# Layer with a clipped scan on one core: the D term written into PSUM by VectorE, the product ring widened, and one buffer for x and the residual

## The chip, the cores and the metric

The kernel runs on one core of one Trainium2 chip. The metric is the device time of one execution in microseconds (us), the median of several runs. The core has a matrix engine (TensorE, PE in the profile; PEld is its weight load), VectorE (DVE), ScalarE (ACT), GpSimd (POOL) and SyncE (SP), which here only issues DMAs. They work side by side, each in its own order of instructions, and wait for one another on semaphores.

## The reference

Input x is 2 x 2048 x 512. Each sequence goes through the same layer, and the result is added to x:

```python
xr, gate = jnp.split(x @ W_in.T, 2, axis=-1)          # 1024 channels each
xr = xr + t_emb[:, None, :]
xc = silu(causal_conv_of_4_taps(xr) + b_conv)
xn = (xc - mu) / jnp.sqrt(var + 1e-05) * ln_g + ln_b
Bm, Cm, dt = jnp.split(xn @ W_xproj.T, 3, axis=-1)    # 16 states each
dt = jnp.tanh(dt @ W_dt.T + b_dt) * 0.01
A = -jnp.tanh(A_log)
Ad = 1.0 + dt * A
Bd = Bm * jnp.minimum(jnp.linalg.norm(xn, axis=-1, keepdims=True), 1.0)
def step(h, inputs):                                   # over 2048 time steps
    h = jnp.clip(h * ad[:, :, None] + bd[:, :, None] * xt[:, None, :], -10.0, 10.0)
    yt = jnp.einsum('bd,bdh->bh', ct, h)
y = ys + D * xn
return x + y * jax.nn.silu(gate) @ W_out.T
```

The change touches the line of `D * xn`.

## The kernel before

Time is cut into 32 chunks of 128 steps (`STEPS`), the two sequences in turn. Body `k` works on chunk k and, beside it, finishes chunk k-1 and prepares chunks k+1 and k+2. A body has 32 steps `s` (`TILES`), one for each pair of a block of 128 channels (`u`, 8 of them) and a group of 4 states (`q`, 4 of them). A tile goes through the engines as follows. TensorE writes the unclipped states into a bank of `ps_fill` (`fill`, L542, three steps ahead), ScalarE copies them to `low` (L779), TensorE adds the width of the clip (`widen`, L551), VectorE runs the clipped scan from `low` and the bank into `ks` (L990), GpSimd multiplies by C into `prod` (`weigh`, L1088), and TensorE adds the product into `ps_y`, transposed (`flip`, L578, `LAG` = 4 steps behind). `ps_y` is a single bank of 512 channels. Tiles 0 to 15 make the first half of y, tiles 16 to 31 the second. Flips 0 and 1, and 16 and 17, are issued as pairs in steps 5 and 21.

A half of y begins with `base` (L558), a matmul with `start=True`. The D term is added by `skip` (L564): GpSimd multiplies xn by D into `xd`, which shares the buffer of `xc` (L1045, after tile 11), and TensorE adds each half of `xd` through the identity, the first half at flip 12, the second at flip 16. Each of these f32 matmuls is two records in the trace. After flips 15 and 31 VectorE multiplies the bank by the gate (`gated`, L978). The next `base` waits for that (`y_gated`). A product buffer of the ring `prod` (`HOLD` = 4) is written again only after its flip.

Beside the tiles TensorE works off jobs. Step s has two points, 2s (before its flip) and 2s+1 (behind it). The table `JOBS`, written by hand, gives for each job the first point, the number of points over which it is spread, the chunk and the bank of `ps_job` (the last number). `TAKE` gives the point at which ScalarE or VectorE empties the bank, and a job waits until the one before it on its bank has been taken. The jobs are: z, zT and nb (the small projections), gate and xr (the input projection), conv and xt, h0, hend and carry (states between chunks), yT (the gated y transposed) and out (the output projection). The carry jobs end in ScalarE's copies to `xh` and `lend` (L755, L757) and VectorE's `xl` (L970), which frees the bank. `GATED_AT` gives the points of the two gate products on VectorE.

SP issues all DMAs in one order: x transposed into `xf` at the body's start (wanted by ScalarE at point 13, step 6), the residual into `res` at once behind it (wanted at point 53), then the stacks, C and bounds, and at the end the store of the chunk from `res`.

## Time and profile before

| | us |
|---|---|
| median of 3 runs | 2132.08 |
| lowest and highest | 2129.33, 2132.22 |
| the profiled execution's own time | 2132.36 |
| its span | 2130.6 |
| its PE busy | 1991.3 |
| its POOL busy | 1799.5 |
| its DVE busy | 1659.2 |
| its ACT busy | 1421.1 |

The profile is of one execution. Busy times of TensorE contain the overlap of one matmul's tail with the next, so the chain of waits, which walks from start to start, shows smaller steps than the durations of the instructions. A release named "issue" is idle time for which the profile shows no other engine.

### The profile page before, as it was taken

Reading aid. Unit: us, or ns where it says so; the run is one execution under the profiler, and the core shown is the slowest. Engines: PE = TensorE matmul, PEld = TensorE weight load, DVE = VectorE, ACT = ScalarE, POOL = GpSimd, SP = SyncE. Lnnn points to the kernel's source line nnn. Section 1 sums busy time; section 2 is a strip of 40 time slices with the busy share of each in tenths; the row PEclk is TensorE's granted clock in tenths of the full one; section 3 lists DMA queues with packets and bytes.
Section 4 is the critical chain, followed back from the end, with each engine's and each line's share of the span. In section 5 each row is a group of like instructions: output and inputs, shape, how many; then the busy total and the mean of one; then the engine's idle time right before and its main releaser. Section 6 shows DMA issues by size and latency. Waiting matters only on the chain.

```text
span 2130.6 us, 47194 instructions
## 1 busy us (share of the span) xinstructions
PE 1991.3 (93%) x16976; PEld 1471.4 (69%) x16976; DVE 1659.2 (78%) x2108; ACT 1421.1 (67%) x3462; POOL 1799.5 (84%) x1444
## 2 busy tenths in 40 slices
PE   5699999999999999999999999999999999999988
PEld 5466777776777776777776777676676777677765
DVE  3477887787887787887787888787888787888796
ACT  4676766776766676766676766676766677766643
POOL 1389898888898888898888898888898888898886
PEclk8699999999999999999999999999999999999999
DMA  5121112121112121112111111211111112121110
GB/s 171 54 59 49 53 43 60 57 61 49 53 42 61 57 59 50 54 44 60 56 58 50 54 50 54 57 56 54 51 57 47 57 56 58 47 59 44 54 49 16
DMA packets 81993, 118.09 MB, mean 55 GB/s; under 512 B 21840, under 2 KB 50896, under 8 KB 77088
## 3 DMA queue, kind: packets, MB, share of 16 engines
q1 hardware_dynamic: 81760, 115.07, 18.7%
q8 instruction: 135, 2.21, 0.4%
q14 instruction: 98, 0.80, 0.1%
HBM read 59.96 MB, written 9.18 MB: 32 GB/s over the span
## 4 chain that ended last, share of the span: by engine, by line
PE 69%; ACT 17%; issue 8%; DVE 4%; POOL 1%; SPq 1%; DMA 0%; ACTq 0%; DVEq 0%; POOLq 0%
PE ps_y L578 13%; PE ps_job L493 8%; PE ps_fill L551 8%; PE ps_job L447 8%; PE ps_fill L542 7%; PE ps_job L452 7%; PE ps_job L465 5%; ACT low L779 4%; PE ps_y L558 3%; PE ps_job L459 2%; PE ps_job L474 2%; ACT tap L738 2%; ACT xh L672 2%; ACT gate L666 2%; PE ps_y L564 1%
## 5 line engine op out<-in xcount | busy, mean ns | idle before, releaser
L1088 POOL TENSOR_TENSOR prod<-ks,crep 128x512 f32<-128x512 f32 x1024 | 1283.6, 1272 | 226.4 <-PE ps_y L578 214.9
L990 DVE TENSOR_TENSOR_SCAN ks<-low,ps_fill 128x512 f32<-128x512 f32 x1024 | 1211.5, 1205 | 228.6 <-PE ps_fill L551 224.6
L779 ACT COPY low<-ps_fill 128x512 f32<-128x512 f32 x1024 | 585.4, 581 | 540.6 <-PE ps_fill L542 536.4
L578 PE MATMUL ps_y<-c_sb,prod 128*128 128x128 f32 x4096 | 610.7, 274 | 2.4 <-POOL prod L1088 1.1
L578 PEld LDWEIGHTS ps_y<-c_sb,prod 128*128 128x128 f32 x4096 | 462.0, 142 | 94.1 <-issue 63.3
L542 PEld LDWEIGHTS ps_fill<-ts,xs 128*128 128x128 f16 x4096 | 316.4, 98 | 165.7 <-issue 5.0
L542 PE MATMUL ps_fill<-ts,xs 128*128 128x128 f16 x4096 | 397.9, 220 | 6.4 <-DVE ks L990 4.2
L551 PE MATMUL ps_fill<-spans,pick 128*128 128x512 f16 x1024 | 391.6, 382 | 9.8 <-ACT low L779 6.8
L738 ACT ACTIVATE tap<-xr,cols_sb 128x128 f32<-128x128 f32 x768 | 252.1, 394 | 16.3 <-PE ps_job L465 16.2
L447 PE MATMUL ps_job<-x,w_in 128*128 128x128 f16 x3072 | 215.7, 221 | 14.6 <-POOL x L1058 7.8
L452 PE MATMUL ps_job<-w_in,x 128*128 128x512 f16 x768 | 209.7, 383 | 10.9 <-ACT gate L666 10.9
L493 PE MATMUL ps_job<-w_out,yT 128*128 128x512 f16 x768 | 206.4, 379 | 1.8 <-DVE yT L901 1.5
L447 PEld LDWEIGHTS ps_job<-x,w_in 128*128 128x128 f16 x3072 | 188.0, 99 | 25.0 <-issue 20.8
L465 PE MATMUL ps_job<-c_sb,tap 128*128 128x128 f32 x1024 | 157.4, 278 | 24.9 <-issue 16.9
L551 PEld LDWEIGHTS ps_fill<-spans,pick 128*128 128x128 f16 x1024 | 100.2, 98 | 74.8 <-ACT low L779 23.5
L465 PEld LDWEIGHTS ps_job<-c_sb,tap 128*128 128x128 f32 x1024 | 118.2, 144 | 42.9 <-issue 22.3
L738 ACT ACTIVATE tap<-xr,conv_b,cols_sb 128x128 f32<-128x128 f32 x256 | 123.5, 482 | 0.0
L452 PEld LDWEIGHTS ps_job<-w_in,x 128*128 128x128 f16 x768 | 71.8, 104 | 48.7 <-issue 17.0
L970 DVE SCALAR_TENSOR_TENSOR xl<-xh,c_sb,ps_job 128x512 f16<-128x512 f16 x64 | 47.8, 747 | 68.8 <-ACT lend L757 68.8
L493 PEld LDWEIGHTS ps_job<-w_out,yT 128*128 128x128 f16 x768 | 69.8, 98 | 35.4 <-DVE yT L901 1.7
L1036 POOL TENSOR_TENSOR xn<-xn,row_g 128x1024 f32<-128x1024 f32 x32 | 75.5, 2359 | 5.5 <-ACT xn L654 5.5
L1045 POOL TENSOR_TENSOR xc<-xn,row_d 128x1024 f32<-128x1024 f32 x32 | 75.4, 2355 | 0.0
(125 smaller groups left out, 2269.7 us busy)
## 6 DMA issues: line engine op xcount, KB each, us to landing
crep<-c_dram SPq DMA_DIRECT2D x32, 1024.0 KB, 4.8
xs<-xh SPq DMA_DIRECT2D x256, 64.0 KB, 2.0
xs<-xl SPq DMA_DIRECT2D x224, 64.0 KB, 2.0
xf<-in_xT SPq DMA_DIRECT2D x32, 256.0 KB, 2.7
res<-in_x SPq DMA_DIRECT2D x32, 256.0 KB, 2.6
out_dram<-res SPq DMA_DIRECT2D x32, 256.0 KB, 2.1
ts<-tth SPq DMA_DIRECT2D x128, 32.0 KB
ts<-tth SPq DMA_DIRECT2D x128, 31.0 KB
```

The source lines that it names most:

```text
L447: last = mm(ps[:, e * P:(e + 1) * P], w_in[:, a, c, d:d + P], x16[:, q, b, c, :], start=(c == n == 0), stop=(c == CB - 1 and n == 2))
L452: last = mm(ps, x16[:, q, a, c, :], w_in[:, b, c, DI + i * BANK:DI + (i + 1) * BANK], start=(c == n == 0), stop=(c == CB - 1 and n == 2))
L465: last = mm(ps[:, e * P:(e + 1) * P], tap[:, d % TAPRING, v], ident, start=(v == 0), stop=(v == TAPS - 1), is_transpose=True)
L493: last = mm(ps, yT[:, a, c, :], w_out[:, b, c, :], start=(c == n == 0), stop=(c == DB - 1 and n == 2))
L542: last = mm(o[:, :, SUB * jj:SUB * (jj + 1)], xs[:, p, jj, u * P:(u + 1) * P], ts[:, p, jj, q * QN * SUB:(q + 1) * QN * SUB].rearrange("s ...
L551: mm(ps_fill[:, (TILES * k + s) % RING], pick[:], spans[:, p, q * BANK:(q + 1) * BANK], start=False, stop=True, skip_group_check=True).the ...
L578: last = mm(ps_y[:, cut], prod[:, s % HOLD, e, :], ident, start=False, stop=(u % 4 == 3 and q == 3 and e == QN - 1), is_transpose=True)
L738: last = act_fn(tap[:, d % TAPRING, v], xr[:, p, d, v:v + P], ACT.Identity, scale=cols[:, d, 3 + v:4 + v], bias=conv_b[:, p, d:d + 1] if v ...
L779: copy(low[:, (TILES * k + s) % RING], ps_fill[:, (TILES * k + s) % RING]).then_inc(sem["low_copied"], 1)
L990: nc.vector.tensor_tensor_scan(ks[:, u % 2, QN * q:QN * (q + 1)].rearrange("d n t -> d (n t)"), low[:, g % RING], ps_fill[:, g % RING], 0. ...
L1036: tt(xn[:, p], xn[:, p], row_g[:], ALU.mult).then_inc(sem["xg"], 1)
L1088: tt(prod[:, i % HOLD], ks[:, u % 2, part], crep[:, p, part], ALU.mult).then_inc(sem["weighed"], 1)
```

## The change

The D term is written by VectorE. A new `skip` on VectorE multiplies half of xn by D and writes the result straight into `ps_y`, right behind each gate product (points 39 and 8); TensorE's `base` waits for it (`skip_set`) and adds to it with `start=False`. One matmul of zeros at the program's start opens the bank. GpSimd's product, the buffer `xd` and TensorE's two skip matmuls are gone. `HOLD` is 5, and the ring is counted through all chunks. In steps 5 and 21, the jobs of the second point come before the pair of flips and the base. `res` is a view of `xf`: the load of x waits for the store before it, the residual's load for `xT_low`, and it moves behind the xl stack loads in SP's order. Some jobs move in the tables.

```diff
-HOLD = 4
+HOLD = 5
-        xd = xc
-        res = sb("res", [P, DM])
+        res = xf[:].rearrange("p c t -> p (c t)")
...
-        TAKE = {("z", 0): 5, ("gate", 0): 7, ("hend", 0): 6, ("hend", 1): 8, ("yT", 1): 10, ("gate", 1): 12,
+        TAKE = {("z", 0): 5, ("gate", 0): 7, ("hend", 0): 6, ("hend", 1): 7, ("yT", 1): 12, ("gate", 1): 12,
...
-        GATED_AT = (39, 7)
+        GATED_AT = (39, 8)
...
+                    if k >= 2:
+                        sp.wait_ge(sem[f"out_done{p}"], 16 * ((k - p) // 2))
                     sp.dma_start(xf[:], xT_dram[b, :, :, bass.ds(c * P, P)]).then_inc(sem["xT_in"], 16)
...
+                if exists(k, -1):
+                    b, c = chunk(-1)
+                    if exists(k, 2):
+                        sp.wait_ge(sem["xT_low"], k + 3)
+                    elif k >= 2:
+                        sp.wait_ge(sem[f"out_done{p}"], 16 * ((k - p) // 2))
+                    sp.dma_start(res, x_dram[b, bass.ds(c * P, P), :]).then_inc(sem["res_in"], 16)
...
+            mm(ps_y[:], pick[:], spans[:, 0, 0:BANK], start=True, stop=True).then_inc(sem["y_opened"], 1)
...
-                since(pe, "y_gated", 2 * k + i)
-                mm(ps_y[:], mT[:, p], xn[:, p, half], start=True, stop=False)
-
-            def skip(k, p, i):
-
-                if i == 0:
-                    pe.wait_ge(sem["xd_done"], k + 1)
-                last = mm(ps_y[:], ident, xd[:, i * BANK:(i + 1) * BANK], start=False, stop=False)
-                if i == 1:
-                    last.then_inc(sem["xd_used"], 1)
+                pe.wait_ge(sem["skip_set"], 2 * k + i + 1)
+                mm(ps_y[:], mT[:, p], xn[:, p, half], start=False, stop=False, skip_group_check=True)
...
+                    if len(tiles) == 2:
+                        jobs_at(k, p, 2 * s + 1)
...
+            def skip(k, p, i):
+
+                half = slice(i * BANK, (i + 1) * BANK)
+                dve.wait_ge(sem["xn_done"], k + 1)
+                since(dve, "y_gated", 2 * k + i)
+                if k == i == 0:
+                    dve.wait_ge(sem["y_opened"], 1)
+                tt(ps_y[:], xn[:, p, half], row_d[:, half], ALU.mult).then_inc(sem["skip_set"], 1)
...
                             gated(k, p, 0)
+                            skip(k, p, 1)
...
-                        tt(xd[:], xn[:, p], row_d[:], ALU.mult).then_inc(sem["xd_done"], 1)
```

The other moved jobs, by their first points: yT 1 from 10 to 12, carry 0 from 32 to 33, carry 1 from 36 to 38, out from 40 in 13 parts to 42 in 12, yT 0 from 54 to 56, hend 1 from 8 to 7.

What that makes of TensorE's order in steps 19 to 21, first before. The rows begin behind the second carry job and flip 14 (`ps_y<-c_sb,prod` is a flip, `ps_job<-c_sb,tap` a part of conv, `ps_job<-w_out,yT` of out, `ps_fill<-spans,pick` a widen and `ps_fill<-ts,xs` a fill).

```order
L551 MATMUL ps_fill<-spans,pick 128x512
L542 MATMUL ps_fill<-ts,xs 128x4x32 x4
L465 MATMUL ps_job<-c_sb,tap 128x128 x4
L578 MATMUL ps_y<-c_sb,prod 128x128 x4
L551 MATMUL ps_fill<-spans,pick 128x512
L542 MATMUL ps_fill<-ts,xs 128x4x32 x4
L465 MATMUL ps_job<-c_sb,tap 128x128 x4
L493 MATMUL ps_job<-w_out,yT 128x512 x3
L551 MATMUL ps_fill<-spans,pick 128x512
L542 MATMUL ps_fill<-ts,xs 128x4x32 x4
L558 MATMUL ps_y<-xn,mT 128x512
L564 MATMUL ps_y<-xc,c_sb 128x512
```

The same steps of the changed kernel, from the end of the second carry job on:

```order
L483 MATMUL ps_job<-xh,bqm 128x512
L572 MATMUL ps_y<-c_sb,prod 128x128 x4
L555 MATMUL ps_fill<-spans,pick 128x512
L546 MATMUL ps_fill<-ts,xs 128x4x32 x4
L469 MATMUL ps_job<-c_sb,tap 128x128 x4
L555 MATMUL ps_fill<-spans,pick 128x512
L546 MATMUL ps_fill<-ts,xs 128x4x32 x4
L469 MATMUL ps_job<-c_sb,tap 128x128 x4
L497 MATMUL ps_job<-w_out,yT 128x512 x3
L562 MATMUL ps_y<-xn,mT 128x512
L572 MATMUL ps_y<-c_sb,prod 128x128 x8
```

The wait of out (before: ahead of the conv part that precedes L493; after: ahead of the one that precedes L497) now stands behind two widens and fills and a conv part that stood in part behind it, and the skip is gone.

TensorE in steps 3 to 5, before, from flip 31 on (`ps_job<-w_in,x` is gate, `ps_job<-c_sb,kend` hend, `ps_job<-c_sb,gate` yT):

```order
L578 MATMUL ps_y<-c_sb,prod 128x128 x4
L551 MATMUL ps_fill<-spans,pick 128x512
L542 MATMUL ps_fill<-ts,xs 128x4x32 x4
L452 MATMUL ps_job<-w_in,x 128x512 x3
L483 MATMUL ps_job<-c_sb,kend 16x128 x4
L452 MATMUL ps_job<-w_in,x 128x512 x3
L551 MATMUL ps_fill<-spans,pick 128x512
L542 MATMUL ps_fill<-ts,xs 128x4x32 x4
L452 MATMUL ps_job<-w_in,x 128x512 x3
L487 MATMUL ps_job<-c_sb,gate 128x128 x4
L558 MATMUL ps_y<-xn,mT 128x512
```

and after:

```order
L572 MATMUL ps_y<-c_sb,prod 128x128 x4
L487 MATMUL ps_job<-c_sb,kend 16x128 x4
L555 MATMUL ps_fill<-spans,pick 128x512
L546 MATMUL ps_fill<-ts,xs 128x4x32 x4
L456 MATMUL ps_job<-w_in,x 128x512 x6
L555 MATMUL ps_fill<-spans,pick 128x512
L546 MATMUL ps_fill<-ts,xs 128x4x32 x4
L456 MATMUL ps_job<-w_in,x 128x512 x6
L562 MATMUL ps_y<-xn,mT 128x512
```

Hend 1 is ahead of the gate job, yT 1 comes after the base, and the gate's fourth part before it.

VectorE from the scans of step 18 to its step 21, before and after (`ks<-low,ps_fill` is a scan, `gate<-ps_y,gate` the gate product, `ps_y<-xn,row_d` the new skip):

```order
L970 SCALAR_TENSOR_TENSOR xl<-xh,c_sb,ps_job 128x512
L990 SCALAR_TENSOR_TENSOR ks<-low,ps_fill 128x512 x2
L970 SCALAR_TENSOR_TENSOR xl<-xh,c_sb,ps_job 128x512
L990 SCALAR_TENSOR_TENSOR ks<-low,ps_fill 128x512
L978 TENSOR_TENSOR gate<-ps_y,gate 128x512
L990 SCALAR_TENSOR_TENSOR ks<-low,ps_fill 128x512 x5
```

```order
L967 SCALAR_TENSOR_TENSOR xl<-xh,c_sb,ps_job 128x512
L996 SCALAR_TENSOR_TENSOR ks<-low,ps_fill 128x512 x2
L975 TENSOR_TENSOR gate<-ps_y,gate 128x512
L984 TENSOR_TENSOR ps_y<-xn,row_d 128x512
L967 SCALAR_TENSOR_TENSOR xl<-xh,c_sb,ps_job 128x512
L996 SCALAR_TENSOR_TENSOR ks<-low,ps_fill 128x512 x5
```

The gate product and the skip now stand ahead of the second xl.

## Rows read from the trace of the kernel before

**Rows 1.** The page: busy time by engine, and the chain by engine.

```profile
PE 1991.3 (93%) x16976; PEld 1471.4 (69%) x16976; DVE 1659.2 (78%) x2108; ACT 1421.1 (67%) x3462; POOL 1799.5 (84%) x1444
PE 69%; ACT 17%; issue 8%; DVE 4%; POOL 1%; SPq 1%; DMA 0%; ACTq 0%; DVEq 0%; POOLq 0%
```

**Rows 2.** Waits (total us, times, longest), then the base's line (durations, first and last).

```profile
ACT low L779 <- PE ps_fill L542: 536.4, 439, 5.0
...
PE ps_y L558 <- DVE gate L978: 1.7, 2, 1.4
...
L558 PE MATMUL ps_y<-xn,mT x128: 592/593/697, 109.8 to 2098.3; 128*128 128x512 f32 x128
```

**Rows 3.** Busy us by stretch: PE, PEld, DVE, ACT, POOL, clock, DMA share.

```profile
998.70:1062.70 64.00, 61.39 (x533) 45.50 (x532) 51.40 (x66) 43.92 (x108) 56.45 (x47) 1.00 0.20 55
...
1018.00:1031.50 13.50, 12.17 (x88) 8.24 (x86) 11.43 (x15) 13.22 (x36) 10.63 (x10) 1.00 0.27 89
```

**Rows 4.** Groups (busy us, mean ns), then min/median/max ns of two VectorE lines.

```profile
L564 PE MATMUL ps_y<-xc,c_sb 128*128 128x512 f32 x128 | 65.4, 593 | 1.2 <-POOL xc L1045 1.2
L978 DVE TENSOR_TENSOR gate<-ps_y,gate 128x512 f32<-128x512 f32 x64 | 42.8, 669 | 0.1
L990 DVE TENSOR_TENSOR_SCAN ks<-low,ps_fill 128x512 f32<-128x512 f32 x1024 | 1211.5, 1205 | 228.6 <-PE ps_fill L551 224.6 <-issue 0.2
L1088 POOL TENSOR_TENSOR prod<-ks,crep 128x512 f32<-128x512 f32 x1024 | 1283.6, 1272 | 226.4 <-PE ps_y L578 214.9 <-DVE ks L990 11.3
L1045 POOL TENSOR_TENSOR xc<-xn,row_d 128x1024 f32<-128x1024 f32 x32 | 75.4, 2355 | 0.0
...
L910 DVE TENSOR_TENSOR zm<-z,zm x32: 178/801/805, 55.6 to 2023.5; 1x32 f16<-1x32 f32 x32
...
L945 DVE TENSOR_TENSOR bc<-zT,pf x32: 403/587/2007, 63.0 to 2033.1; 16x256 f32<-16x256 f32 x32
```

**Rows 5.** Chain of waits, 1028 to 1033 us: start, step, what.

```profile
1028.48 0.65 PE ps_job L493 x3
1029.13 0.21 PE ps_fill L551
1029.34 0.22 PE ps_fill L542 x4
...
1030.64 0.86 PE ps_y L564 x2
1031.50 0.88 PE ps_y L578 x8
```

**Rows 6.** Timeline, TensorE, 1027 to 1034 us: start, duration, [idle before].

```profile
1027.85 0.63 PE L465 MATMUL ps_job<-c_sb,tap 128*128 128x128 f32 x4 [0.59 <-issue]
...
1033.30 0.38 PE L551 MATMUL ps_fill<-spans,pick 128*128 128x512 f16 x1
```

**Rows 7.** Timeline, ScalarE and VectorE in the same steps.

```profile
1017.93 0.59 ACT L779 COPY low<-ps_fill 128x512 f32<-128x512 f32 x1 [0.81 <-PE ps_fill L542]
...
1026.30 0.57 ACT L757 COPY lend<-ps_job 16x512 f32<-16x512 f32 x1
...
1023.37 0.75 DVE L970 SCALAR_TENSOR_TENSOR xl<-xh,c_sb,ps_job 128x512 f16<-128x512 f16 x1 [1.42 <-ACT lend L757]
...
1027.01 0.75 DVE L970 SCALAR_TENSOR_TENSOR xl<-xh,c_sb,ps_job 128x512 f16<-128x512 f16 x1 [0.65 <-ACT lend L757]
```

**Rows 8.** Timeline at the chunk's head.

```profile
999.01 0.58 ACT L660 CAST yT<-ps_job 128x512 f16<-128x512 f32 x1 [0.50 <-PE ps_job L487]
...
1000.42 3.73 POOL L1088 TENSOR_TENSOR prod<-ks,crep 128x512 f32<-128x512 f32 x3 [1.43 <-PE ps_y L578]
...
1003.39 0.80 DVE L910 TENSOR_TENSOR zm<-z,zm 1x32 f16<-1x32 f32 x1 [0.56 <-ACT zm L685]
...
1006.30 0.10 PEld L551 LDWEIGHTS ps_fill<-spans,pick 128*128 128x128 f16 x1 [0.28 <-ACT low L779]
...
1059.28 0.81 PE L452 MATMUL ps_job<-w_in,x 128*128 128x512 f16 x3 [0.34 <-ACT gate L666]
```

More of the change, by code:

```diff
@@ L198, in build @@
         JOBS = [(3, 2, "z", 0, 1, 1, 1), (3, 4, "gate", 0, 0, 2, 0), (6, 1, "hend", 0, -1, 2, 1),
-                (8, 4, "gate", 1, 0, 2, 0), (8, 1, "hend", 1, -1, 2, 1), (10, 1, "yT", 1, -1, 2, 1),
+                (8, 4, "gate", 1, 0, 2, 0), (7, 1, "hend", 1, -1, 2, 1), (12, 1, "yT", 1, -1, 2, 1),
                 (15, 1, "zT", 0, 1, 1, 1), (19, 4, "xr", 0, 2, 2, 0), (21, 1, "h0", 0, 1, 2, 1),
                 (24, 4, "xr", 1, 2, 2, 0), (24, 1, "h0", 1, 1, 2, 1), (27, 1, "nb", 0, 1, 1, 1),
-                (33, 11, "conv", 0, 2, 2, 0), (32, 1, "carry", 0, 1, 2, 1), (36, 1, "carry", 1, 1, 2, 1),
-                (40, 13, "out", 0, -1, 1, 1), (46, 9, "conv", 1, 2, 2, 0), (54, 1, "yT", 0, 0, 2, 1),
+                (33, 11, "conv", 0, 2, 2, 0), (33, 1, "carry", 0, 1, 2, 1), (38, 1, "carry", 1, 1, 2, 1),
+                (42, 12, "out", 0, -1, 1, 1), (46, 9, "conv", 1, 2, 2, 0), (56, 1, "yT", 0, 0, 2, 1),
                 (57, 1, "xt", 0, 2, 2, 0), (60, 1, "xt", 1, 2, 2, 0)]
         LAST = {(name, i): first + parts - 1 for first, parts, name, i, *_ in JOBS}
-        TAKE = {("z", 0): 5, ("gate", 0): 7, ("hend", 0): 6, ("hend", 1): 8, ("yT", 1): 10, ("gate", 1): 12,
+        TAKE = {("z", 0): 5, ("gate", 0): 7, ("hend", 0): 6, ("hend", 1): 7, ("yT", 1): 12, ("gate", 1): 12,
                 ("zT", 0): 15, ("h0", 0): 21, ("h0", 1): 24, ("xr", 0): 23, ("nb", 0): 27,
-                ("xr", 1): 28, ("carry", 0): 32, ("carry", 1): 36, ("conv", 0): 44, ("out", 0): 53,
-                ("conv", 1): 55, ("yT", 0): 54, ("xt", 0): 58, ("xt", 1): 62}
+                ("xr", 1): 28, ("carry", 0): 33, ("carry", 1): 38, ("conv", 0): 44, ("out", 0): 54,
+                ("conv", 1): 55, ("yT", 0): 56, ("xt", 0): 58, ("xt", 1): 62}
         TAP_AT = [24, 26, 32, 36, 39, 42, 45, 49]
         Z_AT = 12
-        GATED_AT = (39, 7)
+        GATED_AT = (39, 8)
         BANK_OF = {(name, i): b for _, _, name, i, _, _, b in JOBS}
@@ L321, in body @@
                     later_loads()
-                if exists(k, -1):
-                    b, c = chunk(-1)
-                    if not (isinstance(k, int) and k < 2):
-                        sp.wait_ge(sem[f"out_done{p}"], 16 * ((k - p) // 2))
-                    sp.dma_start(res[:], x_dram[b, bass.ds(c * P, P), :]).then_inc(sem["res_in"], 16)
                 if exists(k, 1):
@@ L394, in body @@
                     sp.wait_ge(sem["out_taken"], k)
-                    sp.dma_start(out[b, bass.ds(c * P, P), :], res[:]).then_inc(sem[f"out_done{b}"], 16)
+                    sp.dma_start(out[b, bass.ds(c * P, P), :], res).then_inc(sem[f"out_done{b}"], 16)
             steps(body)
@@ L414, in _ @@
             pe.wait_ge(sem["gw_ready"], 2)
+            pe.wait_ge(sem["spans_clear"], 3)
             for i, src in enumerate((gw, bw)):
@@ L572, in flip @@
                     base(k, p, s // (4 * NQ))
-                if s in (3 * NQ, 4 * NQ):
-                    skip(k, p, s // NQ - 3)
                 pe.wait_ge(sem["weighed"], TILES * k + s + 1)
@@ L577, in flip @@
                 for e in range(QN):
-                    last = mm(ps_y[:, cut], prod[:, s % HOLD, e, :], ident, start=False,
-                              stop=(u % 4 == 3 and q == 3 and e == QN - 1), is_transpose=True)
+                    last = mm(ps_y[:, cut], prod[:, (TILES * k + s) % HOLD, e, :], ident, start=False,
+                              stop=(u % 4 == 3 and q == 3 and e == QN - 1), is_transpose=True,
+                              skip_group_check=True)
                 last.then_inc(sem["flipped"], 1)
@@ L609, in body @@
                             flip(k - 1, 1 - p, t + TILES)
-                    jobs_at(k, p, 2 * s + 1)
+                    if len(tiles) < 2:
+                        jobs_at(k, p, 2 * s + 1)
             steps(body)
@@ L743, in side @@
                     since(act, "xa", k + 2)
-                    since(act, "xd_used", k + 1)
                     act_fn(xc[:, i * BANK:(i + 1) * BANK], bank("conv", i), ACT.Silu).then_inc(sem["conv_taken"], 1)
@@ L906, in side @@
                     dve.wait_ge(sem["res_in"], 16 * k)
-                    stt(res[:], bank("out"), 1 / WS, res[:], ALU.mult, ALU.add).then_inc(sem["out_taken"], 1)
+                    stt(res, bank("out"), 1 / WS, res, ALU.mult, ALU.add).then_inc(sem["out_taken"], 1)
                 if point == Z_AT + 1 and exists(k, 1):
@@ L1003, in body @@
                             gated(k, p, 0)
+                            skip(k, p, 1)
                         if point == GATED_AT[1] and exists(k, -1):
                             gated(k - 1, 1 - p, 1)
+                        if point == GATED_AT[1] and exists(k, 0):
+                            skip(k, p, 0)
                         side(k, p, point)
@@ L1087, in weigh @@
                 since(pool, "flipped", g - HOLD + 1)
-                tt(prod[:, i % HOLD], ks[:, u % 2, part], crep[:, p, part], ALU.mult).then_inc(sem["weighed"], 1)
+                tt(prod[:, g % HOLD], ks[:, u % 2, part], crep[:, p, part], ALU.mult).then_inc(sem["weighed"], 1)
             steps(body)
```

6 lines of the change are left out of this document (1 added, 5 removed).

## The prediction

> **What bounds the kernel now.** I read the page first, then the waits, the busy time by stretch, the chain of waits, and the timeline of one chunk. The page puts TensorE at 93%, and the chain that ended last is 69% TensorE and 17% ScalarE [rows 1]. The waits say the same from the other side: ScalarE waits 536 us for the fills of TensorE [rows 2], and VectorE 225 us for its widening matmuls [rows 4]. So TensorE is late and the others wait for it. The first and last base matmul stand at 109.8 and 2098.3 us, 31.5 chunks apart, so a chunk takes 63.1 us [rows 2]. The chunk that I read closely runs from 998.7 to 1062.7 us. In it TensorE is busy for 61.4 us of 64 at the full clock (1.00), GpSimd 56.5, VectorE 51.4, ScalarE 43.9 [rows 3]. No other engine has a full chunk of work, but each has full stretches. From 1018 to 1031.5 us ScalarE is busy 13.22 us of 13.5 and TensorE only 12.17 [rows 3]. What a cut on TensorE is worth has to be read there, and at the chunk's head.
>
> **The D term leaves TensorE.** A skip matmul is recorded as two instructions; the chain walks over the pair in 0.86 us (the 593 ns of one record overlap the next) [rows 4, 5]. Two skips in each of 32 chunks: 64 x 0.86 = 55 us, or 1.72 us a chunk. The order of the changed kernel shows none left, so this work is certainly gone. Whether the time goes too is taken stretch by stretch, for one chunk.
>
> **Tail, steps 16 to 21: -1.6 us.** ScalarE starts this run when a fill arrives at 1017.93 (it had waited 0.81 us) and is busy until it has written the second lend, at 1026.30 plus about half a microsecond [rows 7]. VectorE then makes the second xl at 1027.01, having waited 0.65 us for it, and only that frees the bank for out [rows 7]: TensorE resumes at 1027.85 after 0.59 us of waiting [rows 6]. The first skip stands inside this run, so removing it alone moves nothing past 1027.85; I keep that time for both kernels. What counts is what TensorE still has to do behind it. Before: from 1027.85 to the next widen at 1033.30, 5.45 us [rows 6]: a conv part, an out part, widen and fill, base, skip, two flips, a conv part, an out part. After: out starts at 42 and carry 1 at 38, so the conv part, the widen and the fill come ahead of the wait. Behind it stand a conv part (four transposes, as in a flip) 0.44, an out part 0.65, base 0.86, two flips 0.88, and, one step later, the second out part 0.65: 3.48 us by the steps of the chain, the base taken as long as a skip, which has the same shape [rows 5]. Gain 5.45 - 3.48 = 1.97, say 1.9, since some of the gaps at the base may stay. Thus moved work, not the first skip's absence as such, is what turns the saving into time.
>
> Against it stands VectorE's new order: gate, skip, and only then the second xl. VectorE's gate product takes 0.67 us [rows 4]. No row shows a 128x512 product of two SBUF tensors into PSUM. Lower bound: the gate product's 0.67, also 512 elements. Upper bound: two SBUF inputs seem to wait for GpSimd. The 1x32 zm takes 178 ns at best and 801 ns at the median, the 16x256 bc 403 at best, 587 at the median and 2007 at worst [rows 4]. In the chunk read, the three products that GpSimd began at 1000.42 end at 1004.15 and zm, begun at 1003.39, ends at 1004.19 [rows 8]. One whole product of 1.27 us [rows 4] in front makes 1.94 us. I take the middle, 1.3 us, since GpSimd is busy 56 of 64 us and an instruction meets it half way through on average. Now the place of the skip: the first xl frees the bank at 1023.37 + 0.75 [rows 7]; carry 1 (0.65) and flip 15 (0.44) follow, so flip 15 ends near 1025.4, the gate product near 1026.1 and the skip near 1027.4. The lend ends near 1027.1 (1026.30 plus 0.57 and its signal) in both kernels: xl starts 0.3 us later. Tail: -1.9 + 0.3 = -1.6 us.
>
> The Trainium skill has a rule on this ("SBUF — State Buffer", section "SBUF: two separate sides"): a VectorE op with two SBUF inputs and a GpSimd op that reads SBUF exclude each other for the whole instruction, where sharing would cost only a part. The end of zm with GpSimd's products agrees. By the rule at its worst case the sum would be rival (c)'s.
>
> **Head, steps 3 to 10: +0.15 us.** Count from the end of flip 31. TensorE after: hend 1 0.44, widen and fill 0.43, two gate parts 1.30, widen and fill 0.43, two gate parts 1.30: it asks for the base at 3.9 us. Hend 1 now stands ahead of the gate job, where TensorE waited 0.34 us for ScalarE [rows 8], and fills that: -0.34. VectorE has in that time: the wait for hend 1 (0.6, with the tail of a matmul), then each row's duration less some 0.06 us of overlap: its h product 0.6 (512 elements like the gate product), scan 5 1.15, gate 0.6 [rows 4], and the skip 1.3: 4.25 us, with its signal 4.3. So the base waits 0.4 us; with the skip at 0.67 it doesn't wait, at 1.94 it waits 1.0. Before, the base waited only in 2 of 64 places, 1.7 us in all [rows 2]: this is the wait the change adds. Behind it stand the flips, and GpSimd's products behind them. The yT 1 job leaves this stretch (-0.44) for step 6, and its ScalarE cast (0.58 us, in a place where ScalarE was idle afterwards [rows 8]) goes to the front of a run that ends in TensorE's wait for a low copy at 1006.30, 0.28 us [rows 8]. That run grows by about the 0.5 us of the cast: +0.1 net. Sum: -0.34 + 0.4 + 0.1 = +0.16.
>
> **The rest, each at nothing, and its cover.** GpSimd loses a 2.36 us product a chunk [rows 4] and gains at most two blocks of 0.67 us by the skips; it is not on the chain (1%) [rows 1]. The fifth product buffer lets it run one product, 1.27 us, ahead across the base; flips waited for products too rarely to gain by it. The xT load now waits for the store of the block before, and is wanted only in step 6 of the next chunk; the residual load goes behind the xl stack loads, in step 7, and is wanted in step 27. The SP queue is held at neither, since their conditions were met by the waits ahead of them; were it held, the c and bound transfers behind would be late. Putting yT 0 at 56 and its VectorE half behind the statistics shifts 0.6 us between steps without adding any. The opening matmul happens once.
>
> **Sum.** -1.6 + 0.16 = -1.44 us a chunk; x 32 = -46 us. From the profiled execution's own 2132.36 us (median of the runs 2132.08, so no correction): 2086 us, -2.2%.
>
> **Rivals.** (a) The first skip's time is lost: ScalarE's run slips behind TensorE's new start, or out's wait is reached no later relative to it, and only 0.86 us of the pair comes through. Then -0.58 us a chunk, 2114 us. For it: 13.22 of 13.5 us busy. Against: the jobs moved ahead of the wait. (b) More comes back: VectorE's skips at 0.67 us (no 0.3, no 0.4), giving -2.1 us, 2064 us, and with half of the gap of 0.59 us at out gone too [rows 6], 2055. (c) Nothing: both skips meet a whole product, 1.94 us. Then the tail gains 0.95 and the base at the head waits 1.0: -0.2 us a chunk, 2126 us. That is also what the skill's rule of whole-instruction exclusion gives if each skip comes just behind a product's start. (d) Slower: the D term as a link in the y chain. If each skip takes what the worst bc took, 2.0 us, plus 0.3 for twice the elements (half of the gate's 0.67), the base waits 1.4 us and xl is 1.3 us late: -1.9 + 1.3 - 0.24 + 1.4 = +0.56 us a chunk, 2150 us. It decides from a skip of about 2.0 us on. Against it: bc's median is 0.59, and near the base GpSimd often waits for flips.  That the change doesn't do what it says is excluded by the order.
>
> **Chances.** The forecast's case, 2070 to 2102, 58%; (a) 16%; (b) 12%; (c) 6%; (d) 8%. The range takes in the forecast, most of (a) and the upper part of (b): 2062 to 2118. A difference of 0.2% (4 us) is about what the runs can tell. Faster by more than that 86%, within it 6% ((c) in its upper part, or with a little more of a wait), slower 8%.
>
> **What would show it.** TensorE's busy time down by about 55 us in its lines; VectorE up by 64 skips, 43 us if free and 83 us at 1.3 each; GpSimd down 75. The skip's row: near 0.67, 1.3 or 1.9 us decides between (b), the forecast and (c). The waits: base for skip at the head some 0.4 us in each chunk, none at the tail. If the wait at out grows past the 0.59 us, (a) is right. The forecast is wrong if ScalarE's run from 1018 us doesn't keep its length, or if a wait shows at the base of both halves.

## The result and the profile after

The changed kernel is slower. Its median is 2165.4 us (2164.62 to 2165.97, 4 runs) beside 2132.15 us for the kernel before on the same chip (2129.33 to 2132.42). The ratio is 1.016 (95% interval 1.0141 to 1.0176). The profiled execution spans 2164.2 us; its TensorE clock was granted at 0.983 on average. The forecast was 2086 us.

First the page of the changed kernel: busy time by engine, the chain that ended last, and three groups of instructions (busy us, mean ns of one, idle time before them).

```profile
PE 1937.6 (90%) x16849; PEld 1447.2 (67%) x16849; DVE 1751.9 (81%) x2172; ACT 1419.2 (66%) x3462; POOL 1728.9 (80%) x1412
...
PE 64%; ACT 14%; issue 11%; DVE 8%; POOL 1%; SPq 1%; DMA 1%; ACTq 0%; DVEq 0%; POOLq 0%
...
L1091 POOL TENSOR_TENSOR prod<-ks,crep 128x512 f32<-128x512 f32 x1024 | 1284.3, 1276 | 274.2 <-PE ps_y L572 217.5
...
L984 DVE TENSOR_TENSOR ps_y<-xn,row_d 128x512 f32<-128x512 f32 x64 | 108.1, 1688 | 6.6
...
L562 PE MATMUL ps_y<-xn,mT 128*128 128x512 f32 x128 | 72.7, 652 | 28.7 <-DVE ps_y L984 28.7
```

The work moved as planned. TensorE is 54 us less busy than in [rows 1], GpSimd 71 us less, and VectorE 93 us more. But the kernel didn't end earlier: TensorE now waits more than it saved. The skip's mean is 1.69 us; 0.67 would have been free of contention and 1.3 was assumed. The base matmul, which hardly waited before [rows 2], waits 28.7 us.

The waits say where (us in total, times, longest). PE and PEld are two queues of one engine, and a wait usually stands in both; the PE row is the one to add up.

```profile
ACT low L776 <- PE ps_fill L546: 617.2, 462, 7.4
...
PE ps_job L469 <- issue: 64.4, 28, 2.3
...
PE ps_y L562 <- DVE ps_y L984: 28.7, 28, 3.4
...
PE ps_job L491 <- DVE xf L904: 14.7, 31, 0.9
...
PE ps_job L487 <- DVE h L891: 13.1, 31, 0.4
```

ScalarE waits 81 us more for fills than in [rows 2], so TensorE is what is late. TensorE's own waits that are new or longer are four, each in nearly every chunk: 2.3 us ahead of the conv part that stands before out, 0.9 us at the head's base, and two of 0.4 to 0.5 us which the forecast didn't have, at yT (L491) and at hend (L487). A fifth, small one stands at the z job (L474): 0.22 us in 30 chunks, 6.5 us in all; its row is the last of the head's below.

Now the tail, steps 16 to 21 of one chunk, in the timeline (start, duration, idle before and what ended it). The first row is the start of ScalarE's run, and so matches the first of [rows 7]; the others follow in order of time.

```profile
1031.09 0.58 ACT L776 COPY low<-ps_fill 128x512 f32<-128x512 f32 x1 [0.81 <-PE ps_fill L546]
...
1037.20 2.32 DVE L996 TENSOR_TENSOR_SCAN ks<-low,ps_fill 128x512 f32<-128x512 f32 x2
...
1039.44 0.67 DVE L975 TENSOR_TENSOR gate<-ps_y,gate 128x512 f32<-128x512 f32 x1
...
1039.60 0.57 ACT L754 COPY lend<-ps_job 16x512 f32<-16x512 f32 x1
...
1040.12 1.27 POOL L1091 TENSOR_TENSOR prod<-ks,crep 128x512 f32<-128x512 f32 x1
...
1040.21 1.75 DVE L984 TENSOR_TENSOR ps_y<-xn,row_d 128x512 f32<-128x512 f32 x1
...
1041.87 0.74 DVE L967 SCALAR_TENSOR_TENSOR xl<-xh,c_sb,ps_job 128x512 f16<-128x512 f16 x1
...
1042.71 0.63 PE L469 MATMUL ps_job<-c_sb,tap 128*128 128x128 f32 x4 [2.31 <-issue]
...
1045.55 0.38 PE L555 MATMUL ps_fill<-spans,pick 128*128 128x512 f16 x1
```

The second lend starts 8.51 us after the run's start, 8.37 us before: ScalarE's run kept its length. Its data are there at about 1040.2, but VectorE is in the skip, and xl comes at 1041.87 without having waited for anything. Before, VectorE had waited 0.65 us for the same lend [rows 7]. GpSimd's product at 1040.12 starts 0.09 us ahead of the skip, and the skip ends 0.57 us behind that product's end at 1041.39. TensorE resumes 11.62 us after the run's start; before it was 9.92 us [rows 6, 7]. From there to the next widen it takes 2.84 us (1045.55 - 1042.71) where it took 5.45 [rows 6].

The head, steps 3 to 10 of the same body:

```profile
1007.17 0.60 PE L487 MATMUL ps_job<-c_sb,kend 128*16 128x128 f32 x4 [0.42 <-DVE h L891]
...
1010.30 1.82 DVE L984 TENSOR_TENSOR ps_y<-xn,row_d 128x512 f32<-128x512 f32 x1
...
1010.30 1.26 POOL L1091 TENSOR_TENSOR prod<-ks,crep 128x512 f32<-128x512 f32 x1
...
1012.17 1.13 PE L562 MATMUL ps_y<-xn,mT 128*128 128x512 f32 x2 [0.93 <-DVE ps_y L984]
...
1016.59 0.49 PE L474 MATMUL ps_job<-c_sb,z 128*16 128x128 f32 x3 [0.22 <-DVE yT L898]
```

Skip and product start in the same hundredth of a microsecond. The product takes its plain 1.26 us, and the skip takes 1.82: it too ends 0.56 us behind the product's end.

The next chunk's head is the counter-example, one of three in this trace: here the skip started first, by 0.01 us, and GpSimd's product is the one that is stretched.

```profile
1075.09 0.70 DVE L984 TENSOR_TENSOR ps_y<-xn,row_d 128x512 f32<-128x512 f32 x1
...
1075.10 1.80 POOL L1091 TENSOR_TENSOR prod<-ks,crep 128x512 f32<-128x512 f32 x1
```

### The profile page after: what moved, and what is told of

It is laid out like the page before. It is cut to its first block, busy times and chain, and to the rows that moved or that the text cites. A ratio compares the mean times of both kernels' runs of the same rounds, so it can differ in the third digit from the quotient of the medians.

```text
span 2164.2 us, 47005 instructions
## 1 busy us (share of the span) xinstructions
PE 1937.6 (90%) x16849; PEld 1447.2 (67%) x16849; DVE 1751.9 (81%) x2172; ACT 1419.2 (66%) x3462; POOL 1728.9 (80%) x1412
## 4 chain that ended last, share of the span: by engine, by line
PE 64%; ACT 14%; issue 11%; DVE 8%; POOL 1%; SPq 1%; DMA 1%; ACTq 0%; DVEq 0%; POOLq 0%
PE ps_y L572 13%; PE ps_job L497 8%; PE ps_job L451 7%; PE ps_fill L555 7%; PE ps_fill L546 7%; PE ps_job L456 5%; ACT low L776 4%; PE ps_job L469 4%; PE ps_y L562 3%; PE ps_job L463 2%; DVE ps_y L984 2%; PE ps_job L478 2%; DVE ks L996 2%; ACT tap L736 2%; PE ps_job L487 2%
## 5 line engine op out<-in xcount | busy, mean ns | idle before, releaser
L497 PE MATMUL ps_job<-w_out,yT 128*128 128x512 f16 x768 | 209.1, 383 | 3.9 <-DVE xl L967 2.4
L456 PE MATMUL ps_job<-w_in,x 128*128 128x512 f16 x768 | 199.6, 383 | 0.4 <-ACT gate L664 0.4
L984 DVE TENSOR_TENSOR ps_y<-xn,row_d 128x512 f32<-128x512 f32 x64 | 108.1, 1688 | 6.6
L562 PE MATMUL ps_y<-xn,mT 128*128 128x512 f32 x128 | 72.7, 652 | 28.7 <-DVE ps_y L984 28.7
L497 PEld LDWEIGHTS ps_job<-w_out,yT 128*128 128x128 f16 x768 | 70.4, 99 | 38.3 <-issue 3.6
```

Of the source, the lines that this page charges most:

```text
L456: last = mm(ps, x16[:, q, a, c, :], w_in[:, b, c, DI + i * BANK:DI + (i + 1) * BANK], start=(c == n == 0), stop=(c == CB - 1 and n == 2))
L497: last = mm(ps, yT[:, a, c, :], w_out[:, b, c, :], start=(c == n == 0), stop=(c == DB - 1 and n == 2))
L984: tt(ps_y[:], xn[:, p, half], row_d[:, half], ALU.mult).then_inc(sem["skip_set"], 1)
```

## Experiments

**The theory (T1).** A VectorE product of two SBUF tensors and a GpSimd product that reads SBUF exclude each other for a whole instruction. The skip of the tail stands on VectorE ahead of the second xl, xl frees the bank that out needs, and so the blocked skip stops TensorE. The head's skip stops the base. **The rivals.** (T2) It is the place of the skip alone, at any length. (T3) It is the write into PSUM and the wait for it, wherever it stands. (T4) It is the moved jobs, the ring or the shared buffer, and not the D term.

| kernel | median us (range) | ratio to before (95%) |
|---|---|---|
| changed kernel | 2165.4 (2164.62 to 2165.97) | 1.0159 (1.0141 to 1.0176) |
| e1_one_input | 2098.46 (2097.79 to 2098.97) | 0.9847 (0.9833 to 0.9862) |
| e2_skip_behind_xl | 2106.51 (2091.92 to 2107.73) | 0.9870 (0.9837 to 0.9903) |
| e10_one_input_behind_xl | 2083.85 (2082.26 to 2086.04) | 0.9778 (0.9762 to 0.9794) |
| e5_no_d_term | 2080.23 (2079.39 to 2080.83) | 0.9761 (0.9745 to 0.9777) |
| e4_d_term_as_before | 2109.21 (2106.25 to 2110.98) | 0.9897 (0.9882 to 0.9911) |
| e9_ring5_old_tables | 2123.63 (2122.8 to 2125.15) | 0.9964 (0.9951 to 0.9977) |
| e3_old_tables | 2132.64 (2127.58 to 2136.71) | 1.0008 (0.9998 to 1.0017) |
| e7_ring4 | 2169.51 (2166.99 to 2172.31) | 1.0179 (1.0163 to 1.0194) |
| e6_behind_xl_ring4 | 2097.95 (2097.61 to 2098.92) | 0.9843 (0.9829 to 0.9858) |
| v1_add_ring4 | 2109.25 (2107.99 to 2111.53) | 0.9898 (0.9882 to 0.9915) |
| v2_add_behind_xl | 2103.31 (2101.69 to 2104.1) | 0.9868 (0.9853 to 0.9883) |
| e8_two_jobs_moved | 2063.52 (2060.14 to 2064.28) | 0.9679 (0.9665 to 0.9693) |

### One SBUF input

The skip multiplies xn by a constant 0.1 and not by D; its place, its size and its output stay.

```diff
-                tt(ps_y[:], xn[:, p, half], row_d[:, half], ALU.mult).then_inc(sem["skip_set"], 1)
+                tsc(ps_y[:], xn[:, p, half], 0.1, None, ALU.mult).then_inc(sem["skip_set"], 1)
```

> The changed kernel, but VectorE's skip multiplies xn by the constant 0.1 in place of the row of D: one SBUF input instead of two, the same 128x512 into PSUM (so the D term is computed with a wrong D). Theory T1, GpSimd blocks the two-input skip: the skip falls from 1.74-1.82 us to about 0.70, the wait at out from 2.31 us to about 1.2, the wait of the base at the head (0.93 us) goes: about -2.0 us a chunk, 2100 us. Theory T2, the moved jobs themselves lose: skip shorter, waits about the same, 2150 us or more. Theory T3, a VectorE write into PSUM is slow in itself: the skip stays over 1.5 us, no change from 2165 us.

The skip's line in its trace (min, median and max ns, first and last start):

```profile
L984 DVE TENSOR_SCALAR ps_y<-xn x64: 675/695/696, 106.4 to 2060.8; 128x512 f32<-128x512 f32 x64
```

Its timeline where TensorE resumes ahead of out:

```profile
1010.80 0.63 PE L469 MATMUL ps_job<-c_sb,tap 128*128 128x128 f32 x4 [1.25 <-issue]
```

All 64 skips take 0.7 us, although GpSimd is as busy as in the changed kernel. 67 us are gone, 1.05 us for each skip, which is what a blocked one takes above 0.7. The wait at out falls from 2.31 to 1.25 us. This is T1's number; T2 and T3, by which the length of the skip doesn't matter, fall as the main cause. The edit also makes the instruction another one, a product by a constant. That this isn't what shortens it is shown by the product of two tensors itself: it too takes 0.70 us where it starts ahead of GpSimd's product.

### The skip behind xl, with two inputs and with one

The order on VectorE is changed: gate product, xl, skip.

```diff
                         if point == GATED_AT[0] and exists(k, 0):
                             gated(k, p, 0)
-                            skip(k, p, 1)
 ...
                         side(k, p, point)
+                        if point == GATED_AT[0] and exists(k, 0):
+                            skip(k, p, 1)
```

> The changed kernel with one move on VectorE: at point 39 the skip of the second half stands behind the second xl, no longer ahead of it. T1 (the long skip costs where it stands ahead of xl, which frees out's bank): the wait at out falls from 2.31 to about 0.6 us, the base of step 21 then waits about 0.5 us for the skip: -1.3 us a chunk, 2123 us. T2 (moved jobs): 2155 us or more, the wait at out stays over 1.5 us.

59 us are gone, where 42 were expected (2123 us): the base of step 21 doesn't wait for the skip at all. The wait at out is 0.76 us. The skip of the tail now stands further behind GpSimd's product and takes 0.97 us:

```profile
1007.92 1.27 POOL L1092 TENSOR_TENSOR prod<-ks,crep 128x512 f32<-128x512 f32 x1
...
1008.78 0.97 DVE L984 TENSOR_TENSOR ps_y<-xn,row_d 128x512 f32<-128x512 f32 x1
```

It ends 0.56 us behind the product's end, as the skips of 1.75 and 1.82 us do. So the skip waits for that end, whatever it has waited already.

The heads of two chunks of its trace stand below, VectorE's skip and GpSimd's product of the same moment:

```profile
1041.34 0.70 DVE L984 TENSOR_TENSOR ps_y<-xn,row_d 128x512 f32<-128x512 f32 x1
...
1041.35 1.80 POOL L1092 TENSOR_TENSOR prod<-ks,crep 128x512 f32<-128x512 f32 x1
...
1103.43 1.83 DVE L984 TENSOR_TENSOR ps_y<-xn,row_d 128x512 f32<-128x512 f32 x1
...
1103.43 1.27 POOL L1092 TENSOR_TENSOR prod<-ks,crep 128x512 f32<-128x512 f32 x1
```

It is a race of a hundredth of a microsecond. If VectorE wins, the base is on time. If GpSimd wins, the base waits. In the profiled execution, which took 2091.92 us, VectorE lost in six of the chunks; the other three executions took 2106 to 2108. A chunk of this trace takes 63.2 us from head to head where VectorE loses and 62.1 where it wins, so the 15 us would be some 13 more lost races, by estimate. That this is what happened is likely, but those executions have no trace, so it isn't shown.

Both edits together:

> e1 and e2 together: VectorE's skip multiplies xn by 0.1 (one SBUF input, so a wrong D) and the one of the second half stands behind the second xl. T1 (all that VectorE's skip costs is the block by GpSimd and its place ahead of xl): close to e5, which has no D term, 2080 to 2088 us. If the writes into the bank and the wait of the base cost in themselves: 2095 us or more.

That makes a square of four. Skip ahead of xl: 2165.4 us with two inputs, 2098.5 with one. Skip behind xl: 2106.5 and 2083.9. So the place costs 59 us with a blocked skip and 15 us with a free one, and the block costs 67 us ahead of xl and 23 us behind it, where only the head's skip stops TensorE. With the profiled 2091.92 us in place of the median the block behind xl costs 8 us, which fits its six lost races. T2 holds for a quarter of the place's cost.

### No D term, and the D term as it was

In the first kernel the D term is left out altogether, and the base opens the bank with `start=True` after the gate product.

```diff
-                pe.wait_ge(sem["skip_set"], 2 * k + i + 1)
-                mm(ps_y[:], mT[:, p], xn[:, p, half], start=False, stop=False, skip_group_check=True)
+                since(pe, "y_gated", 2 * k + i)
+                mm(ps_y[:], mT[:, p], xn[:, p, half], start=True, stop=False)
```

> The changed kernel with the D term left out altogether (no skip on any engine, the base starts the bank and waits only for the gate product). T1: both waits that hang on the skip go (2.31 to about 0.5 us at out, 0.93 to 0 at the head): about -2.7 us a chunk, 2079 us. T2: over 2130 us, since the moved jobs stay.

This is the floor for any way of making the D term with these tables. The one-input skip behind xl is 3.6 us above it: T3's price for write and wait. The changed kernel is 85 us above it.

In the second kernel the D term is made as before, by GpSimd into `xd` and by TensorE through the identity, but with the new tables, ring and shared buffer.

```diff
+        xd = xc
 ...
+                if s in (3 * NQ, 4 * NQ):
+                    skip(k, p, s // NQ - 3)
 ...
-                tt(ps_y[:], xn[:, p, half], row_d[:, half], ALU.mult).then_inc(sem["skip_set"], 1)
```

> Everything of the change but the D term: tables, five product buffers, jobs ahead of the pair of flips, shared buffer; GpSimd's product and TensorE's two skip matmuls as before. T1: the rest of the change is about neutral, 2120 to 2140 us. T2: the rest of the change is what loses, 2160 us or more.

The rest of the change gains 21 to 23 us, more than the 2120 to 2140 us expected, and moving the D term to VectorE loses 56 (2165.4 - 2109.2). T4 falls. A second number follows: between this kernel and the floor lie 29 us. That is all that the old D term cost once the jobs stood in the new places, 0.9 us a chunk of the 1.72 that its matmuls take.

### The tables and the ring

The changed kernel with the `JOBS`, `TAKE` and `GATED_AT` of the kernel before:

```diff
-                (8, 4, "gate", 1, 0, 2, 0), (7, 1, "hend", 1, -1, 2, 1), (12, 1, "yT", 1, -1, 2, 1),
+                (8, 4, "gate", 1, 0, 2, 0), (8, 1, "hend", 1, -1, 2, 1), (10, 1, "yT", 1, -1, 2, 1),
 ...
-                (33, 11, "conv", 0, 2, 2, 0), (33, 1, "carry", 0, 1, 2, 1), (38, 1, "carry", 1, 1, 2, 1),
-                (42, 12, "out", 0, -1, 1, 1), (46, 9, "conv", 1, 2, 2, 0), (56, 1, "yT", 0, 0, 2, 1),
+                (33, 11, "conv", 0, 2, 2, 0), (32, 1, "carry", 0, 1, 2, 1), (36, 1, "carry", 1, 1, 2, 1),
+                (40, 13, "out", 0, -1, 1, 1), (46, 9, "conv", 1, 2, 2, 0), (54, 1, "yT", 0, 0, 2, 1),
 ...
-        GATED_AT = (39, 8)
+        GATED_AT = (39, 7)
```

> The changed kernel (D term by VectorE, five buffers, shared buffer, jobs ahead of the pair of flips) with the tables of the kernel before: carry 1 at 36 and out at 40, so that the second xl stands ahead of the gate product and the skip, and yT 1 at 10, hend 1 at 8, yT 0 at 54, gate product at 7. T1 (the long skip costs wherever TensorE asks for its product or for what stands behind it): out no longer waits over 0.8 us, but the base of step 21 waits about 1.8 us for the skip, which ends near 1.75 us after the gate product; the two skips gone give 1.7 us back: 2120 to 2145 us. T2 (the moved tables are what loses): 2100 us or less.

It is within 0.2% of the kernel before, and 33 us faster than the changed kernel: with a skip that blocks, the new tables harm. Its skips take some 1.64 us at the head and 1.39 at the tail (1.4 at the median of both), and they stand elsewhere. First the skip's line, then the waits:

```profile
L984 DVE TENSOR_TENSOR ps_y<-xn,row_d x64: 676/1399/3368, 105.6 to 2097.5; 128x512 f32<-128x512 f32 x64
```

```profile
PE ps_job L483 <- DVE xl L967: 34.5, 32, 1.9
PE ps_job L491 <- DVE h L891: 24.0, 32, 2.1
PE ps_y L562 <- DVE ps_y L984: 17.7, 32, 3.9
```

The base waits 0.55 us a chunk, a third of the 1.8 expected. The block shows more at yT (L491), 0.75 us a chunk: VectorE's h product, which frees yT's bank, stands behind the head's skip. In the kernel before this wait is 0.9 us in all.

The second carry's wait for xl, 1.08 us a chunk, is not the block, since the tail's skip stands behind both xl here. In the kernel before, TensorE reaches the same job later, after its first skip matmul, and waits 0.21 us:

```profile
1024.26 0.38 PE L479 MATMUL ps_job<-xh,bqm 128*128 128x512 f16 x1 [0.21 <-DVE xl L970]
```

ScalarE's lend and with it xl come no earlier (VectorE waits 1.42 us for it in both kernels), so the 0.86 us of that matmul return as 0.87 us of waiting. This is what the prediction said of the first skip, that its removal alone moves nothing, and what rival (a) feared for the whole change. So the time near that of the kernel before is a sum: some 2 us a chunk saved by the two matmuls and a shorter wait at out, and as much lost at carry, yT and base.

The other way round, the kernel before with the fifth buffer and the shared x and residual buffer, its tables and its D term kept:

```diff
-HOLD = 4
+HOLD = 5
 ...
-        res = sb("res", [P, DM])
+        res = xf[:].rearrange("p c t -> p (c t)")
 ...
```

> The kernel before with five product buffers and the shared buffer for x and residual, everything else as before (tables, D term by GpSimd and TensorE). If the fifth buffer gives the 21 us that e4 gained over before: about 2110 us. If the moved jobs give them: 2130 us. If the shared buffer costs something: over 2134 us.

Ring and buffer give 8 us; so the moved jobs give about 14 of the 21 to 23, if the two add up.

Then the ring in the changed kernel, from 5 to 4:

```diff
-HOLD = 5
+HOLD = 4
```

> The changed kernel with four product buffers, nothing else. T1: at point 39 the skip comes 0.8 us after flip 15, which has just released a product (19 in place of 20) in either ring, so it is still blocked for about 1.1 us; at the head it falls to 0.70: the wait of 0.93 us for it goes, the 2.31 us at out stay: about 2140 us. If five buffers are the cause of both blocks, both skips take 0.70 us and the time is about 2100 us. If the ring doesn't matter: 2165 us.

This missed by 30 us. The head came out as expected: with four buffers GpSimd stands still there, the skip takes 0.70 us and the base doesn't wait. At the tail the skip takes 1.42 us and TensorE waits 1.98 instead of 2.31. Yet the kernel isn't faster. TensorE's timeline and then the busy times by stretch (us, then PE, PEld, DVE, ACT, POOL, clock, DMA share, GB/s) say why:

```profile
1042.64 0.63 PE L469 MATMUL ps_job<-c_sb,tap 128*128 128x128 f32 x4 [1.98 <-issue]
...
1043.75 1.84 PE L562 MATMUL ps_y<-xn,mT 128*128 128x512 f32 x2
...
1045.38 1.91 PE L572 MATMUL ps_y<-c_sb,prod 128*128 128x128 f32 x8
```

```profile
1041.00:1043.00 2.00, 0.36 (x4) 0.39 (x5) 2.00 (x3) 2.00 (x5) 0.33 (x1) 1.00 0.07 17
1043.00:1046.00 3.00, 3.00 (x11) 1.59 (x10) 1.78 (x2) 1.97 (x7) 0.00 (x0) 0.64 0.15 40
1046.00:1049.00 3.00, 3.00 (x22) 2.36 (x21) 1.22 (x1) 1.20 (x3) 2.41 (x2) 0.80 0.13 35
```

After the wait the base takes 1.84 us, not 1.02, and the two flips 1.91, not 1.04: 1.7 us lost. The granted clock is 0.64 and then 0.80 of full in the stretches behind the wait, so part of them ran at the lower of the two levels, 1.2 GHz. This comes back in some 21 of 31 chunks, and 21 times 1.7 is 36 us: without it the kernel would have come near the 2140 us expected. In the changed kernel, whose wait is longer, it came in 4 of 31. These four are just the four of the 31 in which the head's skip was free and the base of the head didn't wait. Here are the head's skip and the tail's base of one of them:

```profile
944.96 0.70 DVE L984 TENSOR_TENSOR ps_y<-xn,row_d 128x512 f32<-128x512 f32 x1
...
976.23 0.86 PE L469 MATMUL ps_job<-c_sb,tap 128*128 128x128 f32 x4 [2.29 <-issue]
...
978.17 1.89 PE L562 MATMUL ps_y<-xn,mT 128*128 128x512 f32 x2
```

In the kernel with four buffers no head waits at all. So with the long wait at out still there, the 0.93 us saved at the head were paid back behind out. The one-input kernel has no such chunk, so some 7 of the 67 us between it and the changed kernel (4 x 1.7) are this.

The same four buffers with the skip behind xl:

> The skip of the second half behind the second xl, as in e2, and four product buffers instead of five. T1 with the ring: with four buffers GpSimd has to wait for flip 0 or flip 16 one product earlier, so the skip finds it idle more often: the skip at the head takes 0.70 us in nearly all chunks, no wait of the base there, about 2088 us with less spread than e2's 2092 to 2108. Rival: the ring's fifth buffer is worth something on its own (GpSimd ahead): 2105 us or more.

```profile
L984 DVE TENSOR_TENSOR ps_y<-xn,row_d x64: 674/699/2537, 107.4 to 2056.4; 128x512 f32<-128x512 f32 x64
```

At the median the skip isn't blocked at all, as if it had one input. But the kernel stays 14 us above the one-input kernel with five buffers. Of these, 8.8 us are a wait of its h0 job (0.28 us a chunk), which ends 0.1 us behind GpSimd's subtraction for the low half of xn; with five buffers that wait is absent. The fifth buffer has a worth of its own; the expected 2088 us had left it out, and its rival, 2105 us or more, priced it too high.

### GpSimd makes the product, VectorE adds it

VectorE's instruction has one SBUF input here. GpSimd forms D times xn in two halves after tile 11, and VectorE adds each half to the bank just ahead of the gate product. The ring is 4, since the second half needs a buffer.

```diff
+                tt(ps_y[:], ps_y[:], xd[i], ALU.add).then_inc(sem["skip_set"], 1)
 ...
+                            tt(xd[i], xn[:, p, half], row_d[:, half], ALU.mult).then_inc(sem["xd_done"], 1)
```

> D term without a two-input product on VectorE and without TensorE: GpSimd forms D times xn after tile 11 as in the kernel before (in two halves, 2.4 us), and VectorE adds it to the bank ahead of the gate product, with one input from PSUM and one from SBUF; the base starts the bank and waits only for the gate product. Four product buffers, all else as in the changed kernel. T1: the add takes 0.72 us, no block; xl is 0.7 us later than in e5: wait at out about 1.3 us, none or 0.2 us at the head: 2095 to 2105 us. If any VectorE work between flip 15 and xl costs as much as the skip did, over 2140 us.

The second version has the add and the gate product of the first half behind xl.

> v1 (GpSimd forms D times xn, VectorE adds it in PSUM with one SBUF input, four buffers) with the add and the gate product of the first half behind the second xl. T1: the wait at out falls from 1.20 to 0.75 us, the base of step 21 waits 0.2 to 0.4 us for the gate product: 2095 to 2105 us. If that base waits a microsecond or more: 2110 us or more.

```profile
L978 DVE TENSOR_TENSOR ps_y<-ps_y,xc 128x512 f32<-128x512 f32 x32 | 21.5, 673 | 0.0
```

That is the line of one half's add in the first version. It is not blocked: all adds of both versions take 0.66 to 0.69 us. Out waits 1.20 us in the first and 0.76 in the second. The first version's 2109 us lie above the 2095 to 2105 expected; it has the h0 wait of the kernels with four buffers, 8.6 us. Both beat the kernel before, but the add costs GpSimd's time again, VectorE's besides, and the fifth buffer.

### The two unforeseen waits taken out

The kernel with the skip behind xl, and two jobs moved: hend 1 from point 7 back to 8, and yT 0 from 56 to 58.

```diff
-                (8, 4, "gate", 1, 0, 2, 0), (7, 1, "hend", 1, -1, 2, 1), (12, 1, "yT", 1, -1, 2, 1),
+                (8, 4, "gate", 1, 0, 2, 0), (8, 1, "hend", 1, -1, 2, 1), (12, 1, "yT", 1, -1, 2, 1),
 ...
-                (42, 12, "out", 0, -1, 1, 1), (46, 9, "conv", 1, 2, 2, 0), (56, 1, "yT", 0, 0, 2, 1),
+                (42, 12, "out", 0, -1, 1, 1), (46, 9, "conv", 1, 2, 2, 0), (58, 1, "yT", 0, 0, 2, 1),
```

> e2 (skip of the second half behind the second xl) with two more jobs moved, since both now wait for VectorE to hand over their bank (0.45 us at yT 0 and 0.42 us at hend 1 in each chunk of every kernel with the new tables): hend 1 back from 7 to 8, yT 0 from 56 to 58. If these two waits are what the prediction left out, they go or shrink and the time falls by up to 0.87 x 32 = 28 us, to 2064 to 2085 us. If they only hand the time on to the next wait, it stays at 2092 to 2108 us.

2063.5 us, 3.2% faster than the kernel before (0.9679, 0.9665 to 0.9693), with the whole computation. In turn its page, the skip's line, the base's wait, and two places of the timeline:

```profile
PE 1919.1 (93%) x16849; PEld 1447.0 (70%) x16849; DVE 1720.1 (84%) x2172; ACT 1411.5 (69%) x3462; POOL 1740.0 (85%) x1412
```

```profile
L984 DVE TENSOR_TENSOR ps_y<-xn,row_d x64: 701/1350/1652, 107.6 to 2024.1; 128x512 f32<-128x512 f32 x64
```

```profile
PE ps_y L562 <- DVE ps_y L984: 3.6, 3, 2.1
```

```profile
1025.28 1.52 DVE L984 TENSOR_TENSOR ps_y<-xn,row_d 128x512 f32<-128x512 f32 x1
...
1026.71 0.67 DVE L891 SCALAR_TENSOR_TENSOR h<-lend,ps_job 16x512 f32<-16x512 f32 x1
...
1056.22 0.63 PE L469 MATMUL ps_job<-c_sb,tap 128*128 128x128 f32 x4 [0.75 <-issue]
```

The skip is still blocked, some 1.52 us at the head and 0.98 at the tail, and it costs almost nothing: the base waits 3.6 us in all. With hend 1 at point 8 VectorE takes its h product behind the skip, so the head's skip starts without waiting for it. The two profiled executions, 2091.92 us with only the skip behind xl and 2060.14 here, differ by 32 us. The two waits are gone (14.7 + 13.0 us), and the base waits 6 us less (3.6 after 9.6). The gate job's wait of 0.34 us is back, as in [rows 8], 10.7 us in all. That makes 23 us; the other 9 stand in TensorE's busy time (1928.5 to 1919.1 us). Between the medians the gain is 43 us; how much of that is the head's race, which decides nothing here, isn't shown. The time is below the floor of 2080 us, which was taken with the two jobs in the changed kernel's places.

## Why the prediction was wrong, step by step

**The bound and the D term's 55 us: right.** TensorE's busy time fell by 53.7 us and GpSimd's by 71, and the fills are waited for even more. That ScalarE's run from its fill keeps its length was right to 0.14 us. What TensorE has left behind the wait was right too: 2.84 us, where 3.48 less the second out part's 0.65 gives 2.83.

**The wait ahead of out: the main fault.** The step reads "xl starts 0.3 us later". It was 1.7 us (11.62 against 9.92 us from the run's start to out). Two terms of it failed. The skip starts 9.1 us after the run's start and not 8.2 (1040.21 - 1031.09), because two scans of 2.32 us stand before the gate product; I had counted from the flip's end and not from VectorE's queue. And it lasts 1.75 us and not 1.3. Together 1.4 us a chunk. The tail's gain of 1.6 us shrank to 0.2 or 0.3.

**The skip's price: inside its bounds, and the wrong value taken.** The bounds of 0.67 and 1.94 us held nearly all skips (one took 2.62 us); the middle of 1.3 rested on "an instruction meets it half way through on average". That step fails. The two engines don't meet at random: both follow the same scans and flips, and a chunk repeats the one before. In the tail read above GpSimd's product starts 0.09 us ahead of the skip, at the head the two start within 0.03 us. What meets in phase meets in the same phase in nearly every chunk, and the price is near one end: 0.70 or 1.73 to 1.83. The base of the head waits 0.93 us and not 0.4, and 0.5 of the difference is the skip.

**"The rest, each at nothing": two waits of 28 us in all.** Hend 1 was to fill the 0.34 us that the gate job waited. It did, and waits itself 0.42 us, since its bank is emptied by VectorE's h product of hend 0 only just before. Of yT 0 I wrote that it "shifts 0.6 us between steps without adding any"; at its new point its bank is still held by out, until VectorE's residual sum has taken it, 0.45 us. Both are hand-overs of bank 1, and both could have been priced from the order of the jobs on that bank, by what frees it and when. The last experiment removed them, and its time fell by more than these 28 us. The yT 1 job has a third, its bank not yet taken when z comes: 0.22 us a chunk. In the other edits with no price, ring and buffer, no harm was found; they gave 8 us.

**The sum.** Against the forecast a chunk lost 1.3 us in the tail, 0.5 at the base, 0.42, 0.45 and 0.22 at the hand-overs, and ring and buffer gave 0.24 back: 2.7 us. The mean chunk, by the first and last base (109.9 and 2131.3 us, 31.5 chunks), took 64.2 us, 2.5 more than forecast.

**The rivals.** It was (d)'s mechanism, the skip as a link that xl and the base wait for. Its point of decision, "from a skip of about 2.0 us on", was too high: with the skip's later start and the two hand-overs, 1.75 us is enough. It had 8%. Its price at 2.0 us, 2150, was still too low for the same reasons. Rival (c), which is the rule of whole-instruction exclusion at its worst case and gave 2126 us, had nearly the right length of the skip and the wrong start of it. Rival (b), free skips at 2064 us, is the time of the best kernel, 2063.5, but not by free skips: by skips that something else covers. That the numbers agree is chance.

**The signs.** A wait at out past 0.59 us was to speak for (a). It grew to 2.31, but a late xl stretches the same wait, so this sign can't tell (a) from (d). Neither sign of a wrong forecast came: ScalarE's run kept its length, and only the head's base waits. None of the signs asked for the place of the skip in VectorE's order, which decided.

## What to carry to other kernels

Before an instruction moves to another engine, write down the row of instructions there and what stands behind it; here the price was not the 1.75 us but that xl, which frees a bank for TensorE, stood behind them. A link that can be blocked goes behind the short instructions that others wait for. Two engines that follow the same events tend to meet in the same phase every time, so price the block at its ends and not at its mean. And when jobs on a shared bank are moved, list for each what empties the bank before it, and when.
